# Folded weights split into four blocks: two of the four block sums made from PSUM during the fold, with the prologue, the loads and the first steps in another order

## The reference

```python
# layer 0: a 64x64 weight per sample, then an auxiliary memory with a gate
h = einsum('bct,bcd->bdt', x, L0_cond_weights[cond])
scores = (h @ Wq.T @ Wr.T) @ (aux_keys @ Wr.T).T / sqrt(48) + log_rel; top 8 of 256 slots
aux = softmax(query . key / 8 + log_rel over the 8) @ aux_values @ Wvd.T @ Wvu.T
u = clip(0.5 * log1p(var(h)) / mean(log1p(var(h))) + 2.5 * sigmoid(gelu(h @ Wu1.T + bu1) @ Wu2.T + bu2), 0, 5)
x = x + h + sigmoid(w1 * clip((u - 0.5) / 1.5, 0, 1) + bias) * aux        # 0 where the gate is under 0.05
# layer 1: base weight and a LoRA per sample, then a linear layer with a Fourier-decoded update
y = x @ base_weight.T + base_bias + (x @ lora_A[id].T) @ lora_B[id].T
x = x + y @ W_base.T + b_base + 0.5 * irfft-like(y @ enc.T, coefs * masks)
```

## Time and profile before

| | us |
|---|---|
| runs of the kernel | 1554.64, 1556.2, 1556.33 (median 1556.2) |
| profiled execution, its own time | 1553.39 |
| span of its instructions | 1551.2 |
| busy: TensorE, VectorE, ScalarE, GpSimd | 1451.7, 970.8, 885.7, 699.9 |
| mean granted TensorE clock | 0.971 |

### The profile page before, as it was taken

How to read it: one execution, slowest core, us unless ns; L and a number is a source line. 1 busy time by engine, 2 the same in 40 slices (tenths; PEclk the granted TensorE clock), 3 DMA queues, 4 the chain that set the end, 5 groups by cost and what they waited for, 6 DMA issues and landing times.

```text
span 1551.2 us, 28761 instructions
## 1 busy us (share of the span) xinstructions
PE 1451.7 (94%) x7292; PEld 908.5 (59%) x7292; DVE 970.8 (63%) x2746; ACT 885.7 (57%) x1841; POOL 699.9 (45%) x540
## 2 busy tenths in 40 slices
PE   6897999945789999999999999999999999999997
PEld 3676777632446555566655566655556655556664
DVE  5664777877646656665666666656665666666663
ACT  4575666534456666555655555666655655565652
POOL 3664666446344444444444444444444444444440
PEclk9998999976999999999999999999999999999999
DMA  8586555231033323332333333332332223323322
GB/s 293 199 275 227 181 188 181 86 80 42 21 104 99 105 92 94 104 94 90 90 101 98 91 103 98 108 93 90 98 105 90 90 90 107 93 90 107 109 63 75
DMA packets 160951, 176.14 MB, mean 114 GB/s; under 512 B 104851, under 2 KB 123238, under 8 KB 160785
## 3 DMA queue, kind: packets, MB, share of 16 engines
q1 hardware_dynamic: 156118, 161.56, 33.5%
q10 hardware_dynamic: 4795, 14.15, 2.7%
HBM read 135.97 MB, written 39.32 MB: 113 GB/s over the span
## 4 chain that ended last, share of the span: by engine, by line
PE 76%; issue 7%; POOL 7%; DVE 5%; ACT 2%; SPq 2%; DMA 1%; POOLq 0%; ACTq 0%; DVEq 0%
PE pair L86 19%; PE pair L88 19%; PE pair L87 19%; POOL v_lo L256 7%; PE pair L1650 6%; PE pair L1639 6%; PE pair L1483 2%; DVE m_lo L1710 1%; PE pair L1521 1%; PE pair L1522 1%; PE pair L1528 1%; DMA v_x<-in_x 1%; PE pair L1502 1%; PE pair L1489 0%; PE pair L1511 0%
## 5 line engine op out<-in xcount | busy, mean ns | idle before, releaser
L1363 POOL TENSOR_TENSOR t_narrow<-t_a_raw,t_narrow 128x256 f16<-128x256 f32 x64 | 43.4, 678 | 602.4 <-ACT x_hi L1177 602.4
L256 POOL TENSOR_TENSOR v_lo<-v_x,v_hi 128x1024 fp32r<-128x1024 f32 x64 | 155.5, 2432 | 101.8 <-ACT v_hi L250 101.4
L86 PE MATMUL pair<-m_hi,s_hi 128*128 128x512 f16 x512 | 196.1, 383 | 1.2
L87 PE MATMUL pair<-m_lo,s_hi 128*128 128x512 f16 x512 | 194.9, 381 | 0.0
L88 PE MATMUL pair<-m_hi,s_lo 128*128 128x512 f16 x512 | 194.8, 380 | 0.0
L1386 POOL TENSOR_TENSOR s_lo<-t_xt,s_hi 128x512 f16<-128x512 f32 x128 | 145.1, 1164 | 53.5 <-ACT s_hi L1183 53.5
L86 PE MATMUL pair<-t_narrow,x_hi 128*128 128x352 f16 x512 | 161.1, 315 | 5.8 <-DVE vd L1923 5.7
L87 PE MATMUL pair<-t_narrow,x_hi 128*128 128x352 f16 x512 | 161.1, 315 | 0.0
L88 PE MATMUL pair<-t_narrow,x_lo 128*128 128x352 f16 x512 | 161.1, 315 | 0.0
L1365 POOL TENSOR_TENSOR x_lo<-t_xt,x_hi 128x512 f16<-128x512 f32 x128 | 153.1, 1216 | 0.0
L86 PE MATMUL pair<-m_hi,x_hi 128*128 128x512 f16 x384 | 146.9, 383 | 0.0
(11 more groups left out here) (280 smaller groups left out, 3727.7 us busy)
## 6 DMA issues: line engine op xcount, KB each, us to landing
v_x<-in_x SPq DMA_DIRECT2D x64, 512.0 KB, 3.4
t_xt<-in_x_t SPq DMA_DIRECT2D x64, 512.0 KB, 3.2
out<-t_out_sb SPq DMA_DIRECT2D x64, 512.0 KB, 2.7
rhs_b<-bk_hi SPq DMA_DIRECT2D x256, 64.0 KB, 2.3
t_a_raw<-in_lora_a SPq DMA_DIRECT2D x128, 64.0 KB, 2.8
t_bd<-w_kinds SPq DMA_DIRECT2D x128, 64.0 KB, 2.2
t_rhs_c<-bk_lo SPq DMA_DIRECT2D x128, 64.0 KB, 2.3
blk_raw<-in_left_blocks ACTq DMA_DIRECT2D x10, 512.0 KB, 4.6
```

What stands on the lines that cost most here:

```text
L86: pe.matmul(out, a_hi, b_hi, start=start, stop=False, skip_group_check=skip)
L87: pe.matmul(out, a_hi, b_lo, start=False, stop=False, skip_group_check=skip)
L256: pool.tensor_tensor(v["v_lo"][:, s, :], v["v_x"][:, slot, :], f(v["v_hi"][:, s, :]), ALU.subtract).then_inc(v["v_lo_ready"], 1)
```

## The change

1. **Fold.** ScalarE copies only the left half of each M block. VectorE writes the right half itself, behind its maximum: for the top four chunks PSUM minus the left half, which is T1; for the bottom four PSUM minus T1 of the same column, which is T2. B12 and B22 are not stored. The VectorE loop over pairs becomes two turns and four blocks written out.
2. **Sums.** GpSimd makes T3 = T2 - B11, T4 = T2 - B21 and, in step 1, B22 = T2 + T1. The units come in the order B11, T2, B21, T3, T1, T4, B22.
3. **V.** The left half as before; the right half is Wvu_k B11 + (Wvu_k + Wvu_k+4) T1 + Wvu_k+4 T2, with the sum `wvu_sum` made by GpSimd in the place of wvd_t, so 20 matmuls instead of 16. wvd_t is loaded when V is done. wa_chunks(3) moves behind step 0's first product, and wa_split's two copies (`wa_low`) and three constants (`row_constants`) behind pa_lo of step 0.
4. **Order.** m_high, m_low, split_x(2), sums_high and the log-variance instructions move as the diff shows; in the ready-made part of VectorE's stream (at 1751) only the new order is shown, its lines are the old ones.
5. **Loads.** In setup row tiles 3 and 4 are loaded earlier and w_kinds is stored behind W_base. In the main stage load_x(1) moves ahead of the wait for router_split, load_x(4) and load_x(5) ahead of vb_ready.
6. **Places.** The tiles laid over m32 come in another order, with waits on the units that they overwrite.

Eight leading blanks are left out of each line, and two lines that only add names.

```diff
@@ -165,10 +165,10 @@
         f_["m32"] = tile(passing, "m32", [P, KC, HID], F32, side="right")
-    for name, shape, dt in (("pm_hi1", [P, HID], F32R), ("pm_lo1", [P, HID], F32R),
-                            ("u3", [P, HALF], F32), ("c22", [P, HALF], F32),
-                            ("s16_hi1", [P, 2, HID], F16), ("s16_lo1", [P, 2, HID], F16),
-                            ("rhs_a", [P, HID], F32R), ("rhs_b", [P, 2, HID], F32R)):
+    for name, shape, dt in (("rhs_b", [P, 2, HID], F32R), ("rhs_a", [P, HID], F32R),
+                            ("pm_lo1", [P, HID], F32R), ("pm_hi1", [P, HID], F32R),
+                            ("s16_lo1", [P, 2, HID], F16), ("s16_hi1", [P, 2, HID], F16),
+                            ("u3", [P, HALF], F32), ("c22", [P, HALF], F32)):
@@ -368,18 +368,18 @@
 load_two(kf, "w_base_t", 0, wbase_in)
+load_rows(3)
 sp.dma_start(f_["blk_raw"][:], left_block(t, 0)).then_inc(f_["raw_loaded"], 16)
+load_picked_w(3)
 load_two(kf, "w_base_t", 1, wbase_in)
+sp.dma_start(v["v_x"][:, 0, :], bass.AP(t["x"].tensor, 4 * P * HID, [[HID, P], [1, HID]])
+             ).then_inc(v["x_loaded"][0], 16)
+load_picked_w(4)
+load_two(kf, "w_base_t", 2, wbase_in)
+load_two(kf, "w_base_t", 3, wbase_in)
...
              ).then_inc(g["w_stored"], 16)
-load_rows(3)
-load_picked_w(3)
-load_two(kf, "w_base_t", 2, wbase_in)
-sp.dma_start(v["v_x"][:, 0, :], bass.AP(t["x"].tensor, 4 * P * HID, [[HID, P], [1, HID]])
-             ).then_inc(v["x_loaded"][0], 16)
-load_picked_w(4)
-load_two(kf, "w_base_t", 3, wbase_in)
@@ -684,7 +684,7 @@
     def go(z):
-        act.copy(m32[:, bass.ds(b - LBLK, 1), :].rearrange("p a n -> p (a n)"), z[:]
+        act.copy(m32[:, bass.ds(b - LBLK, 1), LEFT].rearrange("p a n -> p (a n)"), z[:, LEFT]
@@ -822,10 +822,18 @@
-def evac_m(b):
+def evac_m(b, bottom=False):
+    def half(k, cols):
+        return m32[:, bass.ds(k, 1), cols].rearrange("p a n -> p (a n)")
...
     def go(z):
-        return dve.tensor_reduce(g["m_max"][:, bass.ds(b - LBLK, 1)], z[:], AX.X, ALU.max,
-                                 apply_absolute_value=True)
+        dve.tensor_reduce(g["m_max"][:, bass.ds(b - LBLK, 1)], z[:], AX.X, ALU.max,
+                          apply_absolute_value=True)
+        if not bottom:
+            return dve.tensor_tensor(half(b - LBLK, RIGHT), z[:, RIGHT], half(b - LBLK, LEFT), ALU.subtract)
+        dve.wait_ge(s["banks_free"], b - KC // 2 + 3)
+        return dve.tensor_tensor(half(b - LBLK, RIGHT), z[:, RIGHT], half(b - LBLK - KC // 2, RIGHT),
+                                 ALU.subtract)
@@ -839,12 +847,12 @@
 dve.memset(spacer, 0.0).then_inc(s["c_chain"], 1)
-with dve.Fori(0, KC // 2 - 1) as j:
+with dve.Fori(0, KC // 4) as j:
...
     one(b + 1, 1, evac_m(b + 1), const_step)
-one(NB - 2, 0, evac_m(NB - 2), const_step)
-one(NB - 1, 1, evac_m(NB - 1), const_step)
+for b in range(LBLK + KC // 2, NB):
+    one(b, b % 2, evac_m(b, bottom=True), const_step)
@@ -948,18 +957,18 @@
     BLOCKS = B11, T1, B21, T2, T3, T4, B22 = range(7)
-    SUMMED = (T1, T2, T3, T4)
+    SUMMED = (T3, T4, B22)
     HALVES = KC // 4
-    UNITS = [(blk, j) for blk in BLOCKS for j in range(HALVES)]
+    UNITS = [(blk, j) for blk in (B11, T2, B21, T3, T1, T4, B22) for j in range(HALVES)]
...
 top, bottom = slice(2 * j, 2 * j + 2), slice(KC // 2 + 2 * j, KC // 2 + 2 * j + 2)
-if blk in (B11, T1, T2):
+if blk in (B11, T3):
     return m32[:, top, LEFT]
-if blk == T3:
+if blk == T1:
     return m32[:, top, RIGHT]
-return m32[:, bottom, RIGHT] if blk == B22 else m32[:, bottom, LEFT]
+return m32[:, bottom, RIGHT] if blk in (T2, B22) else m32[:, bottom, LEFT]
@@ -1073,6 +1082,7 @@
 sp.dma_start(b["gates"][:, 0:3], t["gate_params"]).then_inc(s["row_in"], 16)
+load_x(1, 1)
@@ -1082,12 +1092,12 @@
 sp.dma_start(b["wu2"][:], t["wu2"]).then_inc(s["row_in"], 16)
-sp.dma_start(wvd_t, t["wvd_t"]).then_inc(s["av_in"], 16)
-load_x(1, 1)
...
 sp.wait_ge(s["wu_split"], 1)
+sp.wait_ge(s["v_mm_ready"], 2)
+sp.dma_start(wvd_t, t["wvd_t"]).then_inc(s["av_in"], 16)
@@ -1102,13 +1112,13 @@
     load_wa(q, q % 2)
+load_x(4, 0)
+load_x(5, 1)
...
 load_adapters(1, 1)
-load_x(4, 0)
-load_x(5, 1)
@@ -1207,9 +1217,11 @@
 last.then_inc(s["const_hi_ready"], 1)
+act.wait_ge(s["powers_ready"], 1)
+m_high(0)
+m_high(1)
...
 a_high(3)
-act.wait_ge(s["powers_ready"], 1)
@@ -1217,9 +1229,9 @@
 act.activation(wq_groups(1, 0), wq_raw(1), ACT.Identity, scale=HQ_SCALE).then_inc(s["wu_hi_ready"], 1)
+m_high(2)
+m_high(3)
 split_x(1, 1)
-m_high(0)
-m_high(1)
@@ -1242,17 +1254,13 @@
         last.then_inc(s["pa_hi_ready"], 1)
-    if isinstance(n, int) and n == 1:
-        m_high(8)
-        m_high(9)
-        act.wait_ge(s["wa_stored"], 16)
-    if p == 1 and (not isinstance(n, int) or n + 2 < NT):
+    if isinstance(n, int) and n == 0:
+        m_high(4)
+        m_high(5)
+    if p == 1 and (not isinstance(n, int) or 1 < n < NT - 2):
...
         sums_high(n, q)
-    if isinstance(n, int) and n == 2:
-        m_high(12)
-        m_high(13)
@@ -1264,12 +1272,16 @@
                        ).then_inc(s["z2_ready"], 1)
-    if isinstance(n, int) and n == 0:
-        m_high(2)
-        m_high(3)
...
         act.copy(p1[:], pm_ps[:, LEFT]).then_inc(s["p1_ready"], 2)
+    if isinstance(n, int) and n == 1:
+        act.wait_ge(s["wa_stored"], 16)
+        split_x(2, 2)
+        m_high(8)
+    if isinstance(n, int) and n == 2:
+        m_high(12)
+        m_high(13)
@@ -1281,10 +1293,6 @@
         if isinstance(n, int) and n == 0:
-            m_high(4)
-            m_high(5)
-            act.wait_ge(s["wa_mm_done"], KC // 2)
-            sums_high(0, 0)
@@ -1300,12 +1308,14 @@
     if second_part(n, q):
+        if isinstance(n, int) and n == 2:
+            act.wait_ge(s["m16_lo_ready"], len(UNITS))
...
     if isinstance(n, int) and n == 0:
-        m_high(6)
-        m_high(7)
+        act.wait_ge(s["wa_mm_done"], KC // 2)
+        sums_high(0, 0)
@@ -1318,12 +1328,16 @@
                        ).then_inc(s["c_hi_ready"], 1)
+    if isinstance(n, int) and n == 0:
+        m_high(6)
+        m_high(7)
     if isinstance(n, int) and n == 1:
+        m_high(9)
...
     if isinstance(n, int) and n == 2:
+        sums_high(2, 2)
         act.wait_ge(s["m16_lo_ready"], len(UNITS))
-        sums_high(2, 2)
@@ -1341,21 +1355,17 @@
     for j in range(HALVES):
-        up, down = slice(2 * j, 2 * j + 2), slice(KC // 2 + 2 * j, KC // 2 + 2 * j + 2)
-        out = m_block(blk, j)
-        if blk == T1:
+        out, t2 = m_block(blk, j), m_block(T2, j)
+        if blk == T3:
             pool.wait_ge(s["m16_lo_ready"], m_units(B11, 2 * j))
-            in0, in1 = m32[:, up, RIGHT], m32[:, up, LEFT]
-        elif blk == T2:
-            pool.wait_ge(s["m16_lo_ready"], m_units(T1, 2 * j))
-            in0, in1 = m32[:, down, RIGHT], m32[:, up, LEFT]
-        elif blk == T3:
-            in0, in1 = m32[:, down, RIGHT], m32[:, up, RIGHT]
+            pool.tensor_tensor(out, t2, m_block(B11, j), ALU.subtract).then_inc(s["t_ready"], 1)
+        elif blk == T4:
+            pool.wait_ge(s["m16_lo_ready"], m_units(B21, 2 * j))
+            pool.tensor_tensor(out, t2, m_block(B21, j), ALU.subtract).then_inc(s["t_ready"], 1)
         else:
-            pool.wait_ge(s["m16_lo_ready"], m_units(B21, 2 * j))
+            pool.wait_ge(s["m16_lo_ready"], m_units(T2, 2 * j))
             pool.wait_ge(s["t_ready"], 3 + j)
-            in0, in1 = m32[:, up, LEFT], m32[:, down, LEFT]
-        pool.tensor_tensor(out, in0, in1, ALU.subtract).then_inc(s["t_ready"], 1)
+            pool.tensor_tensor(out, t2, m_block(T1, j), ALU.add).then_inc(s["t_ready"], 1)
@@ -1387,23 +1397,28 @@
+pool.wait_ge(g["wvu_in"], 16)
+pool.tensor_tensor(wvu_sum, g["wvu_raw"][:, 0:KC // 2, :], g["wvu_raw"][:, KC // 2:, :], ALU.add
+                   ).then_inc(s["wvu_summed"], 1)
+pool.wait_ge(s["v_mm_ready"], 1)
+t_sums(T3)
...
 split_x(1, 1)
-pool.wait_ge(s["v_mm_ready"], 1)
-t_sums(T1)
 sums(0)
-t_sums(T2)
 sums_low(0, 0)
-t_sums(T3)
...
     new = not isinstance(n, int) or n + 2 < NT
+    if isinstance(n, int) and n == 2:
+        pool.wait_ge(s["m16_lo_ready"], m_units(T1, 2))
...
         split_x(n + 1, (q + 1) % 4)
+        if isinstance(n, int) and n == 1:
+            t_sums(B22)
@@ -1418,9 +1433,18 @@
             pe.wait_ge(g["wvu_split"], 1)
-        for h in range(2):
-            c = slice(h * HALF, (h + 1) * HALF)
-            last = pe.matmul(out_ps[:, c], g["wvu_raw"][:, k, :], m32[:, k, c], start=(k == 0), stop=(k == KC - 1))
+        if k < KC // 2:
+            for c in (LEFT, RIGHT):
+                last = pe.matmul(out_ps[:, c], g["wvu_raw"][:, k, :], m32[:, k, LEFT],
+                                 start=(k == 0), stop=False)
+            continue
+        pe.wait_ge(f_["banks_free"], LBLK + k + 3)
+        pe.wait_ge(s["wvu_summed"], 1)
+        pe.matmul(out_ps[:, LEFT], g["wvu_raw"][:, k, :], m32[:, k, LEFT], start=False, stop=(k == KC - 1))
```

(86 more changed lines are left out.)

21 lines of the change are left out of this document (2 added, 19 removed).

## The result

The changed kernel took 1519.1 us (median of four runs, 1517.98 to 1519.9) against 1556.3 of the kernel before (four runs on the same chip): ratio 0.9762 [0.9745, 0.9779], some 37 us faster. The forecast was 1520. The profiled execution took 1518.98 us for a span of 1516.9, against 1551.2 in span before: -34.3, at a mean granted clock of 0.984 instead of 0.971.

What follows compares the result with a forecast made beforehand. TensorE, full in the fold and from 440 us on, was held between them by waits and the lower clock behind them. Terms -3 - 15.4 - 16.0 + 3.0 - 4.7 = -36 against 1556.2 gave 1520 us, range 1509 to 1536.

Steps and rivals of the forecast that it cites:

- A: Prologue loads: row tile 3 issued earlier, w_kinds stored last, so TensorE's wait goes: -3 us (ends -4 and +2).
- B: The fold: VectorE's added subtraction per M block is covered by idle time; nothing, at most 5.5 us.
- C: Fold's end to step 0's mix: pa_lo freed from work queued ahead, mix earlier: -15.4 us (ends -10 and -17).
- D: Step 0's mix to step 1's transpose: 1 of 16.8 us of waits left: -16.0 us (ends -8 and -19).
- E: Steps 1 and 2: new waits on u2 and for u3 and c22: +3.0 us (ends -1 and +10).
- F: Step 3: x(4), x(5) loaded earlier, wait before scores goes, adapters late next: -4.7 us (ends +1 and -8).
- Rival 4: The fold: VectorE's added subtraction stalls TensorE in all 8 blocks, 5 us each: 1560 us; slower by any cause 0.03.
- rival 1: Router, gate chains and m_lo: VectorE and GpSimd keep meeting, 14 us come back: 1534 us; chance 0.20.
- Rival 2: Steps 0 and 1: the clock stays up at 2.4 GHz, work there shrinks: 1512 us; chance 0.11.
- rival 3: Step 2: new waits through the chain T4, B22, cast, low part; 1540 us at 20 us late; chance 0.06.

Runs made afterwards that it cites:

- the full copy: Changed kernel with ScalarE copying all 1024 columns of each M block in the fold again: 1518.0 us, ratio 0.9777 to the kernel before.
- the run with x(1) late: Changed kernel with the load of x(1) back behind step 0's constant rows: 1526.0 us, ratio 0.9827 to the kernel before.
- the run in which it rests: Changed kernel with GpSimd's split of x(1) held until VectorE has cast the router: 1519.6 us, ratio 0.9771 to the kernel before.
- The repeated kernel: The changed kernel measured again, unaltered: 1517.7 us, ratio 0.977 to the kernel before.
- the one with the old prologue order: Changed kernel with setup's loads in the old order (row tiles 3 and 4 late, w_kinds stored early): 1522.5 us, ratio 0.9808 to the kernel before.
- The run with x(4), x(5) late: Changed kernel with the loads of x(4) and x(5) behind the adapters again: 1523.4 us, ratio 0.9829 to the kernel before.
- the split of x(2): Changed kernel with the split of x(2)'s second half back ahead of step 1's tanh: 1517.9 us, ratio 0.9761 to the kernel before.

## Why the prediction was right

The time, the sign and the mechanism came as forecast: the holes before step 0's mix, before step 1's transpose and before step 3's scores were, with the prologue's 6, the stake. Two of its signs failed: u_sb stays in the list of waits with 5.7 us, and u2 cost 5.4 where 1 to 2 were expected. And the sum was right with terms that were off both ways and cancelled.

| term | forecast | measured in the first profile |
|---|---|---|
| A, prologue loads, with B, the fold | -3 and 0 | -6.15 (V at 287.22) |
| C, fold's end to step 0's mix | -15.4 | -12.6 |
| D, mix to step 1's transpose | -16.0 | -18.0 |
| E, steps 1 and 2 | +3.0 | +7.2 |
| F, step 3 and the rest | -4.7 | -4.7 |
| sum | -36 | -34.3 |

- **A** was mis-sized. "That wait should go: -3" held (3.16 became 0.68), and the feared delay of row 5 behind the store of w_kinds, 4.4 us on SP, reached no product. What I left out is the clock behind the wait: 11.68 us of work at 0.80 became 8.87 at 1.00, of which 0.8 went to the longer wait for row tile 4. Its worth is 5.0; the last 1.2 of the 6.15 are the spread of the way to V.
- **B**, nothing, is confirmed: prologue to V 221.6 to 225.2 us in all executions, before 223.9, and the full copy's 3.4 us on ScalarE don't show. Rival 4 is out.
- **C**: the place was right, the size 2.8 us too large, and the step that failed is "before it on VectorE remain six router instructions". Counted from V's first product, the weights' low parts ended at 26.2 (forecast 26.0) and the six took 5.4 us beside GpSimd (forecast 5.1), but between them stand the five log-variance instructions (L1794 to L1799, 313.39 to 316.15), which the change had moved there and I had not counted: 2.8 us, 1.5 of it their own time, as the run with x(1) late shows, where they run from 311.56 to 313.04. GpSimd's share in this stretch, rival 1 in one place, is 3.35 us by the run in which it rests; x(1)'s early load, which brings it there, is worth 3.0 all the same.
- **D**: 1 us of the 16.8 of waits was to be left, and 1.81 are: -15.0. The other 3.0 are work done faster, 14.09 us for 17.09, at a clock of 0.68 instead of 0.55. I had kept the clock out of the middle value of this term. It is a condition of the gain, since 17.09 us of work would not fit into 15.9, and not its measure. The repeated kernel has 0.9 of wait and 15.0 of work, the one with the old prologue order 0.2 and 15.7, and the stretch is 15.9 us in all three, because VectorE, nearly full, sets it. VectorE's row (length, busy time, then clock, DMA share and GB/s), before and after:

```profile
341.05:374.99 33.94, 25.43 (x34) 0.55 0.26 60
```

```profile
322.30:338.20 15.90, 14.98 (x37) 0.68 0.31 51
```

  Before, six m_lo stand in it with 11.7 us, 6.72 of them in the pair beside T3 and T4 of the earlier trace rows; after, four with 6.0.
- **E** is the term that was most wrong. The waits forecast were 1.9 for u2 and 2.5 for c22's and u3's low parts; measured 5.4 and 1.1. I counted ScalarE's queue before tanh, and not that VectorE's gelu, 0.42 alone, and the sum, 0.43 alone, take 1.37 and 2.45 beside GpSimd's split of x(2) and sum B22. Of the miss of 4.2, u2 is 3.5, two short waits that I had not foreseen (t_query, u) 1.0, and the products, 32.9 us for 30.1, 2.7. Against these stand 1.4 less for c22 and u3, 1.0 more of u_sb that came back, and 0.7 that the sum has for exp and that no wait shows. Up to 2.4 of the 7.2 us are the clock of that one profile: equal code lies at +4.7 to +7.2.
- **F**: -4.7 forecast and measured; the adapters, named as late next at 2.1, were so at 2.73 (0.5 before). The 1.2 for rhs_a is no wait in the list, and the work behind the hole gave some 1.0 instead of 1.7, so here too two errors met. The run with x(4), x(5) late puts the moved loads at 6.1, the adapters' loss already taken off.
- **Rival 1**, the two engines keep meeting, came in two of its places: 3.35 us at the router, and in step 1, where B22 beside one sum is worth 2.0 of the wait on u2; of its 14 us that is about 5. **Rival 2**, the clock stays up, came in part: the mean clock is 0.68 from mix to transpose, and in one run of nine 1.00 behind it; **rival 3** didn't come: T4 and B22 are never waited for.

So the sum came out at -34.3 for -36 because errors of -3.2 and -2.0 met +2.8 and +4.2. Open is what decides whether step 1 gets 0.59, 0.78 or 1.00: in six of those nine runs the shorter wait ahead of it goes with the higher clock, but why TensorE's clock from mix to transpose was 0.57, 0.61 or 0.68 in them no run shows. Open is also how the gains of C and D divide between the sums made from PSUM and the new order.

The Trainium skill, "SBUF — State Buffer", section "Who interferes with whom", says that VectorE and GpSimd contend for a shared port when a VectorE instruction has two SBUF inputs and the GpSimd one beside it reads SBUF. The trace agrees in kind: the sum of two SBUF inputs is 2.45 us beside B22 and 0.43 without, and the router's L1807 1.48 and 0.41.

## What to carry to other kernels

Ask of each load moved earlier which engine it wakes, and what that engine then stands beside: x(1)'s early load gave 3 us at the mix and its GpSimd work took 3.35. A wait removed alone can be worth little because another one ends just behind it (0.77 of 3.35 us reached step 1). Where a hole goes, price the work behind it at the higher clock too (2.8 us in the prologue, 1.4 to 3.0 ahead of step 1), and then ask which engine ends the stretch: from mix to transpose it was VectorE, and between 0.57 and 0.68 the clock moved nothing. And before two edits are compared, compare their clocks: the split of x(2) seemed worth 1.1 us and comes out at 2.6 against runs of equal clock.

## What was not expected of the hardware

- Equal code, with equal milestones before it, was granted a clock of 0.59, 0.78 or 1.00 over the same 7.75 us, and step 1 to step 3 took 43.1, 41.6 or 40.7 us with it. What differed ahead of it was the clock from mix to transpose, 0.68, 0.61 or 0.57, and the wait at its end, 1.8, 0.9 or 0.2 us: the run that was faster there was slower behind. So a microsecond saved ahead of such a stretch may or may not be seen at the end: the prologue's old order cost 5.45 us at V's start and 3.8 in the span.
- A VectorE instruction of 256 columns, 0.43 us alone, took 2.45 beside a GpSimd sum of 1024 columns; the short instruction pays in proportion far more than m_lo (1.27 to 1.86 and 2.73).
